# Where the output passes of a down projection hand over: the copy of the first product behind the next weight blocks, and the residual sums behind theirs

## The reference, cut to what matters

```python
def _matmul_lora(x, w, a, b, scale=1.0):
    out = jnp.einsum('bsd,hd->bsh', x, w)
    out = out + jnp.einsum('bsr,hr->bsh', jnp.einsum('bsd,rd->bsr', x, a), b) * scale
    return out
gate = _matmul_lora(x, gate_w, gate_a, gate_b)
up = _matmul_lora(x, up_w, up_a, up_b)
hidden = jax.nn.silu(gate) * up                       # 1024 tokens x 2752
out = _matmul_lora(hidden, down_w, down_a, down_b)    # 1024 tokens x 1024
...
x = x + _L1_ffn_ref(_layernorm(x), ...)               # the kernel's output
```

## Time and profile before

| | |
|---|---|
| median of three runs | 1162.9 us (1162.12 to 1163.22) |
| the profiled execution: its own time | 1162.12 us |
| the profiled execution: its span | 1160.3 us |
| PE busy | 1083.1 us, 93% of the span |
| DVE busy | 914.2 us, 79% |
| ACT busy | 524.1 us, 45% |
| mean granted TensorE clock | 0.984 of full |

### The profile page before, as it was taken

How to read it: one execution, slowest core, us unless ns; L and a number is a source line. 1 busy time by engine, 2 the same in 40 slices (tenths; PEclk the granted TensorE clock), 3 DMA queues, 4 the chain that set the end, 5 groups by cost and what they waited for, 6 DMA issues and landing times.

```text
span 1160.3 us, 16323 instructions
## 1 busy us (share of the span) xinstructions
PE 1083.1 (93%) x6028; PEld 531.6 (46%) x6034; DVE 914.2 (79%) x1830; ACT 524.1 (45%) x815; POOL 155.7 (13%) x183
## 2 busy tenths in 40 slices
PE   4787999899999999969999999999999999999898
PEld 2354554644445444434444444444444444444443
DVE  8998888889994187877888888988787875666665
ACT  6887753773145235744454545444444342121211
POOL 4884350073004010000000000000000000000000
PEclk9997999999999999999999999999999999999989
DMA  9620000123032029774346253424121632313121
GB/s 368 271 100 1 2 1 1 73 76 106 1 109 87 1 69 241 192 137 92 87 119 157 98 154 92 144 84 128 37 100 39 221 138 73 118 55 118 55 82 55
DMA packets 104207, 118.44 MB, mean 102 GB/s; under 512 B 74752, under 2 KB 78976, under 8 KB 104128
## 3 DMA queue, kind: packets, MB, share of 16 engines
q1 hardware_dynamic: 104128, 117.40, 32.8%
HBM read 86.97 MB, written 16.78 MB: 89 GB/s over the span
## 4 chain that ended last, share of the span: by engine, by line
PE 71%; DVE 22%; ACT 3%; issue 2%; DMA 1%; SPq 0%; DVEq 0%; ACTq 0%
PE PAIR L2790 32%; PE PAIR L2888 14%; PE PAIR L2442 6%; PE PAIR L2443 6%; PE PAIR L2444 6%; DVE X L1734 2%; DVE PAIR L1686 2%; PE PAIR L2745 2%; DVE LORA L1685 1%; DVE LORA L1687 1%; DVE POOL L1560 1%; DVE POOL L1867 1%; DVE BST L1532 1%; DVE X L1603 1%; DVE BST L1533 1%
## 5 line engine op out<-in xcount | busy, mean ns | idle before, releaser
L2790 PE MATMUL PAIR<-XT,POOL 128*128 128x512 f16 x1008 | 230.6, 382 | 9.1 <-DMA XT<-POOL 5.4
L2790 PEld LDWEIGHTS PAIR<-XT,POOL 128*128 128x128 f16 x1008 | 98.3, 98 | 126.2 <-issue 13.6
L1129 ACT ACTIVATE POOL<-STG 128x512 f16<-128x512 f32 (+1 forms) x167 | 96.2, 612 | 90.1 <-DVE STG L1975 85.4
L2888 PE MATMUL PAIR<-POOL 128*128 128x512 f16 x528 | 122.9, 389 | 10.7 <-DVE T4B L1998 10.7
L2442 PE MATMUL PAIR<-POOL 128*128 128x512 f16 x336 | 128.4, 382 | 1.6 <-DVE POOL L1777 1.6
L2443 PE MATMUL PAIR<-POOL 128*128 128x512 f16 x336 | 128.3, 382 | 0.0
L2444 PE MATMUL PAIR<-POOL 128*128 128x512 f16 x336 | 128.2, 382 | 0.0
L2790 PE MATMUL PAIR<-X,POOL 128*128 128x512 f16 x504 | 115.7, 379 | 1.4 <-DMA X<-POOL 1.4
L1129 ACT ACTIVATE POOL<-ST 128x512 f16<-128x512 f32 (+1 forms) x64 | 39.5, 617 | 161.1 <-DVE ST L1862 161.1
L1867 DVE TENSOR_TENSOR POOL<-STG,POOL 128x512 f16<-128x512 f32 (+1 forms) x167 | 106.2, 668 | 1.2 <-ACT POOL L1129 1.1
L2888 PEld LDWEIGHTS PAIR<-POOL 128*128 128x128 f16 x528 | 52.0, 100 | 74.4 <-DVE POOL L1867 12.1
(11 more groups left out here) (342 smaller groups left out, 1928.9 us busy)
## 6 DMA issues: line engine op xcount, KB each, us to landing
STG<-in_gate_w SPq DMA_DIRECT2D x21, 512.0 KB, 5.0
STG<-in_up_w SPq DMA_DIRECT2D x21, 512.0 KB, 5.8
STG<-in_ctx_t SPq DMA_DIRECT2D x16, 512.0 KB, 4.3
STG<-in_ctx SPq DMA_DIRECT2D x16, 512.0 KB, 4.1
STG<-in_down_w SPq DMA_DIRECT2D x16, 512.0 KB, 3.9
POOL<-in_ctx SPq DMA_DIRECT2D x12, 512.0 KB, 11.0
X<-in_x SPq DMA_DIRECT2D x8, 512.0 KB, 9.6
xt_keep<-POOL SPq DMA_DIRECT2D x16, 256.0 KB, 3.1
```

Source lines behind the costliest of these rows:

```text
L1129: e.activation(block(j, name)[:, 0, :, :], src, ACT.Copy).then_inc(b_hi, 1)
L2790: i = e.matmul(dst, blk[:, a_, k, :], src[:, b_, k, :], start=(opens and k == 0 and n == 0), stop=(k == KD // 2 - 1 and n == 2), skip_grou ...
L2888: last = e.matmul(dst, blk[:, a_, i - i0, :], src[:, b_, :], start=first, stop=(c == NSET - 1 and i == i1 - 1 and n == 2))
```

## The change

Two things move. No instruction is added or taken away, and no wait is changed.

- On ACT `first_product` now stands behind the seven `block_hi` of the next chunk, where it stood ahead of them. This acts at `d` = 3, 6 and 9. At `d` = 12 no chunk follows, so its place is the same.
- On DVE the two `residual_sum`s now stand together behind the chunk's last `block_lo`, where they stood among its `down_add`s. This acts at `d` = 2, 5, 8 and 11.

```diff
@@ ACT's list
             for d in range(1, CHUNKS + 1):
-                if d % NSET == 0:
-                    first_product(d // NSET - 1)
                 if d < CHUNKS:
                     for name in BLOCKS:
                         block_hi(HT + d, name)
+                if d % NSET == 0:
+                    first_product(d // NSET - 1)
@@ DVE's list
                     down_add(j, 0)
                     down_add(j, 1)
-                    if d % NSET == NSET - 1:
-                        residual_sum(d // NSET, 0)
                     block_lo(j, "A11")
                     down_add(j, 2)
-                    if d % NSET == NSET - 1:
-                        residual_sum(d // NSET, 1)
                     down_add(j, 3)
...
-                if d % NSET == 0:
+                if d % NSET == NSET - 1:
+                    residual_sum(d // NSET, 0)
+                    residual_sum(d // NSET, 1)
+                elif d % NSET == 0:
                     evacuate(d // NSET - 1)
```

## The result

| | kernel before | changed kernel |
|---|---|---|
| median of four runs | 1163.06 us (1162.12 to 1163.74) | 1170.63 us (1168.36 to 1172.22) |
| ratio | 1 | 1.0064, 95% interval 1.0046 to 1.0083 |
| the profiled execution: its own time | 1162.12 us | 1167.87 us |
| its span | 1160.3 us | 1166.1 us |
| mean granted TensorE clock | 0.984 | 0.978 |

The change makes the kernel slower. The forecast was 1167.1 us with a range up to 1169.4 us. The profiled execution came out at 1167.87 us, and is not among the four; the median of the four runs lies 3.5 us above the forecast and outside the range. So there are two things to explain: what the change costs, and why the first four runs a side showed more.

A forecast was written before the change was run, and what follows sets the result against it. The prediction took PE, busy 93% of the span, to bound the kernel. To the profiled 1162.12 us it added 5.0 us at the three hand-overs and 0 for the residual sums and loads: 1167.1 us, range 1164.9 to 1169.4.

The forecast's parts named there:

- PE's gate: At each hand-over between passes, A11 on PE waits for ACT's later copy and starts 5.00 us later than before.
- A12's own wait: PE's 3.58 us wait before A12 for DVE's first `evacuate` instruction at each hand-over; claimed to be gone.
- the fold's wait at the second hand-over: PE's fold waited 0.89 us for DVE's late `down_add` there; claimed to go, leaving a cost of 0.21 us.
- the mark: Time from the old pass's end to the second fold's start after it; 15.59 us claimed at full clock.
- The sum of the marks: Three hand-overs, each 15.59 us plus 2.26 us mean clock loss: 53.55 us, against 48.55 us before.
- The cost of 5.0 us: Whole cost of the change, at the three hand-overs: 53.55 - 48.55 us; 3.3 to 6.7 us by clock loss.
- the clock falling no more often than before: Rival at the hand-overs: clock losses stay as they were; cost 2.7 us, 1164.9 us; chance 0.07.
- the clock staying up: Rival: full clock through all three hand-overs, marks 46.77 us, 1.8 us won, 1160.3 us; chance 0.02.
- the copy as no gate: Rival: A11's start does not depend on ACT's copy, so 1162.1 us as before; chance 0.02.
- the residual sums matter: Rival: earlier `down_add`s on DVE bring the next pass's blocks earlier, up to 4 us in all, about 1163; chance 0.02.
- The longer stretches at half clock: Rival: each PE restart at a hand-over loses about 3.4 us; cost 8.4 us, 1170.5 us; chance 0.10.
- Sure to be caught: Claim that PE's longer unbroken gap, 5.00 us against 3.58, brings the clock down at all three hand-overs.

The follow-up runs named there:

- changed_kept_busy: The changed kernel with 20 matmuls that nobody reads put on PE before A11 at each hand-over; 1163.45 us, ratio 0.9991 to the kernel before.
- sums_move_only: The kernel before with only the residual sums on DVE moved behind the chunk's blocks, the copy left in place; 1164.16 us, ratio 0.9997.
- copy_behind_four: The kernel before with ACT's copy put behind four of the next chunk's seven block copies, ahead of the last three; 1161.97 us, ratio 0.9981.

## Why the prediction was wrong

**What held, step by step.** The copy became PE's gate, with its end 4.85 us and PE's restart 4.99 us after the old pass (forecast 5.00). A12's own wait went, and with it the fold's wait at the second hand-over. Without loss the mark is 15.57 us (forecast 15.59; `changed_kept_busy`). The clock fell at all three hand-overs in each of four profiles, with a mean loss of 2.23 us over 12 hand-overs (forecast 2.26). The sum of the marks was forecast at 53.55; it was 54.04, 53.74 and 52.50 in three profiles of the changed kernel. The residual sums cost nothing, and neither did the loads behind them. The cost of 5.0 us stands against 4.7 us in the two repeated comparisons (intervals from 2.7 to 6.6 us), and 5.49 in the marks of the first pair of profiles. Three rivals fell by the same runs: the clock falling no more often than before, the clock staying up, and the copy as no gate. `sums_move_only` took away the fourth, that the residual sums matter. The longer stretches at half clock (1170.5 us) were not seen: no loss was above 2.89 us, where that rival wanted 3.4. That its time is close to the one measured is chance as far as the profiles tell; the four runs themselves were not profiled. "Sure to be caught" for a longer gap was a step of the prediction's own; the runs show 15 of 15 against 6 of 9.

**What failed** is the step from the cost to a time and its range: the prediction put the start of the first hand-over at the 981.45 us of one execution, for every run of both kernels. In its words: "Part of that spread may be the same clock falling at other hand-overs, which is in my sum already, so I do not add the 0.8 us to it". I put the cost on the fastest execution of three and took the range from the hand-overs alone. But most of the spread between executions does not come from the hand-overs. With the clock's loss there taken out, runs still spanned 4.7 and 8.2 us. The kernel before, over the comparison runs, lay between 1160.22 and 1170.10 us, where the first four had shown 1162.12 to 1163.74. On the base of the median, 1163.06 + 5.0 = 1168.1 us would have been the forecast: 0.9 of the 3.5 us. The other 2.6 us are the difference between the two medians, 7.6 us, and the cost of 5.0.

The profiles say where such microseconds sit. In all twelve of them the span is the start of the first hand-over, plus the three marks, plus 130.3 us, to within 0.05 us. The first hand-over starts between 981.26 us (`copy_behind_four`) and 986.78 (`sums_move_only`). Those 5.5 us lie ahead of everything that the change touches, and the prediction had them at nothing. An estimate from it: the median of 1170.63 us is a span of 1168.8; less 130.3 and the marks of 54.04 it leaves a start at 984.5, 3 us later than in the kernel before's profile and inside what the profiles show.

For the largest difference one can see where it comes in. `sums_move_only` reached its first hand-over at 986.78, the kernel before at 981.45: 5.3 us later, with the same list of instructions up to `d` = 2. Most of it is there by 110 us. The kernel before first, at the same place of the program:

```profile
105.28 0.59 PE L2442 MATMUL PAIR<-XT 128*128 128x512 f16 x1 [3.29 <-DVE XT L1721]
```

```profile
88.50 7.04 DVE L1537 TENSOR_SCALAR SM<-SM 128x4 f32<-128x4 f32 x1
...
98.99 0.82 PE L2548 MATMUL PAIR<-LORA,XT 128*128 128x24 f16 x24 [5.77 <-DVE XT L1597]
...
109.20 0.38 PE L2441 MATMUL PAIR<-XT 128*128 128x512 f16 x1 [2.33 <-DVE XT L1721]
```

There 3.9 us of the 5.3 have come in (109.20 against 105.28), with one wait of 5.77 us that the kernel before does not have. DVE's work in front of it has a row of its own kind: L1537 adds a constant to four numbers in each partition, and takes 7.04 us. In the other eleven profiles no instruction of that line takes more than 0.78 us. It ends at 95.54, 0.03 us behind a group of POOL's instructions (L761, 90.46 to 95.51). What held it was not tried. This is one profile of twelve: in the other eleven the place shown is reached within 1.1 us (105.11 to 106.17), the first hand-over within 3.2 us (981.26 to 984.46). Most of their spread comes in between the two, and where was not read.

**What stays open.** Why the first four runs a side showed 7.5 us and not 4.7 is not settled. The two later comparisons have 8 and 12 runs of the changed kernel beside 25 and 23 of the other, and agree at 1.0040. In the first, all four runs of the kernel before lay in the lower half of the band that it shows elsewhere, and three of the four of the changed kernel were above 1170 us. A draw of that kind is possible but not likely: of four runs taken at random from the changed kernel's later 20 and four from the other's 83, about 1 in 100 give 7.6 us or more. The four runs also show a granted clock of 0.975 to 0.977, at the low end of the 0.975 to 0.984 of the later 20, so they spent more time at the lower level; in which part is unknown, as none of the four was profiled. More clock loss at the hand-overs than in any of the profiles is thus not excluded for these four, and neither is a property of the chip, which is not on record. The later medians, 1169.24 and 1168.47 us, lie inside the forecast's range, but by some luck: the kernel before stood at 1164.8 and 1164.2 us beside them, not at the 1162.12 of the forecast.

## What to carry to other kernels

- A copy that frees a bank belongs on its engine right behind the product that fills it. In a list that is worked through in order, putting it behind copies that are due later makes the next user of the bank wait for all of them, even if the engine is 45% busy.
- What two waits in a row cost is a matter of which ends last. The copy cost nothing behind four block copies and 5 us behind seven; worked out, the point is where the work between the two waits no longer ends before the second (five and six were not run). And where PE waits for the tail of a long chain on DVE, cut the chain and lay its pieces into DVE's own waits: that was worth 16 us.
- Forecast a time from the median of many runs, and give the range at least the spread that the kernel shows between executions. A cost can agree with the repeated runs to about half a microsecond and the time still be 3 us off.

## What the runs showed of the hardware that was not expected

- A gap of 3.58 us on PE brought TensorE's clock down at 6 of 9 hand-overs, gaps of 4.77 to 4.83 us at 15 of 15. A gap of 2.98 us brought it down too, at two of three (`copy_behind_four`): the clock read 0.50 from 985.0 us at the first, where PE had restarted at 984.40. At a hand-over where the clock fell, 1.1 to 2.9 us were lost. The Trainium skill ("TensorE: Matmul & The Clock Gate", section on the HAM clock gate) says that the watch runs free of the program; the trace agrees as far as it goes: equal gaps of 3.58 us in one execution lost 0, 1.68 and 2.83 us.
- Matmuls whose results nobody reads kept the clock up in all six gaps in which they were put (granted clock 1.00 from 960 to 1130 us in both profiles), and the work behind them started no later (4.99 and 6.33 us after the old pass, as without them).
- One DVE instruction on 128x4 elements took 7.04 us in one profile, and at most 0.78 us in eleven others; the program reached the down projection's first hand-over 5.3 us later than in the kernel before's profile.
- Where an instruction waits for two semaphores, the profile named the engine that was busy (DVE's L1867), and not the one whose end released it (ACT's L1215, 0.14 us before the start).
